# First attention: the keys' tiles of the score matmuls 128 columns wide as the stationary operand in place of 126

## The chip, the cores and the metric

The kernel is one program on one core of a Trainium2 chip. The metric is the time of one execution on the device in microseconds (us); lower is better. It was run three times before the change.

## What is computed

Two gated layers of a Flamingo-like block on 8 sequences of 256 tokens (T = 2,048 queries, 256 wide) that attend to 8 x 1,601 = 12,808 context tokens, with 16 heads of 16 dimensions:

```python
x = x + tanh(g_xattn[0]) * L0_xattn(layernorm(x), ctx)
x = x + tanh(g_ffn[0])   * L0_ffn(layernorm(x))      # experts, top 2
x = x + tanh(g_xattn[1]) * L1_xattn(layernorm(x), ctx)
x = x + tanh(g_ffn[1])   * L1_ffn(layernorm(x))
```

The change lies in `L0_xattn`, in which every query of all sequences sees all 12,808 keys:

```python
q, k, v = fq_sym(q * scale, -1), fq_sym(k, -1), fq_sym(v, 2)   # int8 steps
attn = einsum('bhqd,bhkd->bhqk', q, k)
attn = fq_unsigned(softmax(attn), -1)    # rounded to max/255
out  = einsum('bhqk,bhkd->bhqd', attn, v)
```

Rounding to the row's maximum/255 makes the exact maximum of each row of scores necessary before the exponentials: exp(score - maximum + ln 255) is then the unrounded step, and adding 1024 in a 16-bit float rounds it.

## The kernel before, in words

The program goes through its stages one after the other: projections and quantization of queries, keys and values, the first attention (`first_attention`, lines 792 to 1211), its output projection, the first feed-forward layer, the second attention and the second feed-forward layer. Only the first attention is touched.

It goes through 16 heads and, for each, two chunks of 1,024 queries: 32 bodies, written out four at a time (`IB` = 4), the first four flat and the others in a loop `Fori(1, LOOPS)` with `LOOPS` = 8, so seven turns. Within a body the keys are cut into `NE` = 102 tiles of `KT` = 126, the last of 82. The operands:

- `Kb` (`a_K`): keys in bf16, 112 rows (dimensions and their parts), two halves for two heads, 12,808 columns each. Rows 0 to 53 (`E_ROWS`) serve the scores for the exponentials, with six rows that subtract the row's maximum; rows 64 to 111 (`M_ROWS`) serve the scores for the maximum.
- `Qb` (`a_Q`): queries in the same rows, four chunks.
- `e` (`a_e`), `p` (`a_p`): exponentials in fp32 and rounded in fp16, rings of 8 tiles of 126 keys x 1,024 queries.

Work of one step s (one tile of keys), by engine:

- TensorE: two score matmuls (`e_half`, L1047): the tile of keys is stationary, 54 rows x 126 columns, and 512 queries move, one PSUM bank each. Between them one maximum piece each (`m_piece`, L1064): 128 queries stationary, 48 rows, and 512 keys move, for the maximum of the body after. Then the output matmuls of the tile four steps back (`av`): four with the values stationary (L1087, 32 columns, column tiles of the array) and four with `sel` (L1091), which sum the exponentials in fp32.
- VectorE: one reduction to the maximum of each piece (L1180), 200 whole ones and a short one (L1183) a body; then the maximum over them (L1191). The pieces have three PSUM banks.
- ScalarE: one exponential over 1,024 queries (L1151) for each tile.
- GpSimd: the rounding (L918) for each tile; once a body, at step `SPLIT` = 93, six small operations that split the maximum in bf16 parts (L900 to L910).

The order on TensorE is a list that is built once (lines 855 to 873) and issued for each body: for each half of a step the score matmul, then as many pieces as are due (201 over 204 slots, so three slots have none), and behind the second half the output matmuls that are owed. Steps 4 and 5 have no output matmuls, steps 6 and 7 have two tiles of them. After step `TURN` = 98 eight transposes (L1073) turn the next body's maxima, which ScalarE copies to `Qb` (L1136). Waits: a score half waits until the exponential two tiles back is done, since scores have two pairs of banks (L1046); a piece waits for the reduction three pieces back (L1062); output matmuls wait for the rounding (L1080); the first of a body waits for ScalarE's copy of the previous body's output (L1083, L1132).

Before the first piece TensorE waits for GpSimd's four memsets (L879 to L883, `init`).

Of the kernel before, what the change touches and what calls it, by code (L numbers as in the profile page):

```python
# [8 lines left out]
BF16 = mybir.dt.bfloat16  # L9
# [5 lines left out]
P = 128  # L15
BANK = 512
HEADS = 16
HD = 16
# [19 lines left out]
M_AT, IROWS = 2 * HD, 6  # L38
E_ROWS = 3 * HD + IROWS
M_ROWS = slice(64, 64 + 3 * HD)  # L40
# [45 lines left out]
class Kernel:  # L86
# [705 lines left out]
    def first_attention(self):  # L792


        nc, sh = self.nc, self.sh
        NE, NM, NC, KT, QC, QT, PIECES = sh.NE, sh.NM, sh.NC, sh.KT, sh.QC, sh.QT, sh.PIECES
# [10 lines left out]
        LN255 = math.log(255.0)  # L807
        K_DMAS, Q_DMAS, O_DMAS = 9, 6, 8
        with ExitStack() as ctx:
            Kb = self.sb(ctx, "a_K", [M_ROWS.stop, 2, sh.NK], BF16)  # L810
            Qb = self.sb(ctx, "a_Q", [M_ROWS.stop, 4, QC], BF16)
            Vb = self.sb(ctx, "a_V", [P, 2, sh.KTILES, 2 * HD], F16)
            skb = self.sb(ctx, "a_sk", [P, 2, sh.KTILES])
# [9 lines left out]
            init = self.sem(ctx, "a_init")  # L823

            ld_k = [self.sem(ctx, f"k_loaded{b}") for b in range(2)]
# [15 lines left out]
            def e_bank(i, s):  # L841

                return 2 * ((i + s + (s > TURN)) % 2)
# [6 lines left out]
            def key_rows(t):  # L850
                return sh.KLAST if t == sh.KTILES - 1 else KT
# [6 lines left out]
            for slot in range(2 * NE):  # L858
                s, y = divmod(slot, 2)
# [15 lines left out]
            @block.gpsimd  # L875
            def _(g):
                for s in self.early_sems:
                    g.sem_clear(s)
                g.memset(mparts[:, :, :], 0.0).then_inc(init, 1)  # L879
                g.memset(sel[:, 0:HD], 0.0).then_inc(init, 1)  # L880
                g.memset(sel[:, HD:2 * HD], 1.0).then_inc(init, 1)
                g.wait_ge(init, 3)
                g.memset(p[96:P, :, :], SHIFT).then_inc(init, 1)  # L883
                g.wait_ge(init, 4)

                def held(sem, value):
                    g.wait_ge(sem, value)
                    g.sem_inc(pool_held, 1)

                def split(it, ii, first=False):  # L890

                    n, hb, t0 = it * IB + ii, (ii // NC) % 2, (ii % NC) * QT
                    c = n * LINKS
                    cols = mparts[:, :, M_AT:M_AT + IROWS].rearrange("p t (a b) -> p t a b", b=2)
                    hi, mid, lo = cols[:, :, 0:3, 0], cols[:, :, 0:2, 1], cols[:, :, 2, 1]
                    held(ld_k[hb], 16 * K_DMAS * (it + ii // NC // 2 + 1))
                    held(m_ready, n + 1)
                    if not first:
                        held(m_turned, n)
                    g.tensor_tensor(ms[:, 1, :], ms[:, 0, :], sqb[:, hb, t0:t0 + QT], ALU.mult).then_inc(chain, 1)  # L900
                    held(chain, c + 1)
                    g.tensor_scalar(ms[:, 2, :], ms[:, 1, :], -1.0, LN255, ALU.mult, ALU.add).then_inc(chain, 1)
                    held(chain, c + 2)
                    g.tensor_copy(hi, along(ms[:, 2, :], 2, 3)).then_inc(chain, 1)
                    held(chain, c + 3)
                    g.tensor_tensor(ms[:, 3, :], ms[:, 2, :], hi[:, :, 0], ALU.subtract).then_inc(chain, 1)
                    held(chain, c + 4)
                    g.tensor_copy(mid, along(ms[:, 3, :], 2, 2)).then_inc(chain, 1)
                    held(chain, c + 5)
                    g.tensor_tensor(lo, ms[:, 3, :], mid[:, :, 0], ALU.subtract).then_inc(m_split, 1)  # L910
                    held(m_split, n + 1)

                def body(it, i):
                    for s in range(NE):
                        kk = i * NE + s
                        rows = key_rows(s)
                        held(exp_done, it * (IB * NE) + kk + 1)
                        g.tensor_scalar(p[0:rows, kk % RE, :], e[0:rows, kk % RE, :], 1.0, SHIFT,  # L918
                                        ALU.mult, ALU.add).then_inc(rounded, 1)
                        if s == SPLIT:  # L920
                            held(rounded, it * (IB * NE) + kk + 1)
                            split(it, i + 1)
                split(0, 0, True)
                for i in range(IB):
                    body(0, i)
                with g.Fori(1, LOOPS) as it:
                    for i in range(IB):
                        body(it, i)
# [4 lines left out]

            def load_k(sp, h, b, at):
                row, part = (M_KEYS + E_KEYS)[at]
                sp.dma_start(Kb[row:row + HD, b, :], self.d_k0[part, h]).then_inc(ld_k[b], 16)

            def load_inv(sp, h, b):
                sp.dma_start(Kb[M_AT:M_AT + IROWS, b, :], self.d_inv[h]).then_inc(ld_k[b], 16)

            def load_v(sp, h, b, at):
                r = slice(at * P // V_DMAS, (at + 1) * P // V_DMAS)
# [94 lines left out]
            def _(pe):  # L1037
                def e_half(g, i, s, y, first_body):
                    n, kk = g * IB + i, i * NE + s
                    if y == 0:  # L1040
                        if s == 0:
                            pe.wait_ge(m_rows, n + 1)
                        if s == TURN + 2:
                            pe.wait_ge(m_rows, n + 2)
                        elif not (first_body and kk < 2):
                            pe.wait_ge(exp_done, g * (IB * NE) + kk - (s != TURN + 1))  # L1046
                    last = pe.matmul(self.PS[0:key_rows(s), e_bank(i, s) + y, :], Kb[0:E_ROWS, (i // NC) % 2, s * KT:s * KT + key_rows(s)],  # L1047
                                     Qb[0:E_ROWS, i % 4, y * BANK:(y + 1) * BANK], start=True, stop=True)
                    if y == 1:
                        last.then_inc(scores_e, 1)  # L1050
# [57 lines left out]
                        elif not first_body:  # L1108
                            av(g - 1, IB - 1, op[2], False)

                pe.wait_ge(init, 4)
                for j in range(NM):
                    m_piece(0, 0, 0, j, True)
                m_turn(0, -1, 2)
# [10 lines left out]
            @block.scalar  # L1125
            def _(a):
                def gather(n, b, o_used):

                    a.wait_ge(av_done, (n + 1) * NE)
                    if o_used is not None:  # L1130
                        a.wait_ge(o_stored[b], o_used)
                    a.activation(og[:, b, :], self.PS[:, O_BANK, 0:QW], ACT.Copy).then_inc(gathered, 1)  # L1132

                def rows(n, b, bank):
                    a.wait_ge(m_turned, n + 1)
                    a.activation(Qb[M_AT:M_AT + IROWS, b, :], self.PS[M_AT:M_AT + IROWS, bank, :].bitcast(BF16),  # L1136
                                 ACT.Copy).then_inc(m_rows, 1)

                def body(g, i, first_body):
                    n = g * IB + i  # L1140
                    hb = i // NC
                    for s in range(NE):
                        kk = i * NE + s
                        if s == 0 and i % NC == 0:
                            a.wait_ge(ld_k[hb], 16 * K_DMAS * (g + 1))
                        a.wait_ge(scores_e, g * (IB * NE) + kk + 1)
                        if s % 2 == 0 and not (first_body and kk < RE):

                            a.wait_ge(av_done, g * (IB * NE) + kk - RE + 2)
                        r = key_rows(s)  # L1150
                        a.activation(e[0:r, kk % RE, :], self.PS[0:r, e_bank(i, s):e_bank(i, s) + 2, :], ACT.Exp,  # L1151
                                     scale=skb[0:r, hb, s:s + 1]).then_inc(exp_done, 1)

                        if s == LAG + 1 and not (first_body and i == 0):
                            if first_body and i <= 2:
                                gather(n - 1, (i - 1) % 2, None)
                            elif i > 0:
                                gather(n - 1, (i - 1) % 2, 8 * O_DMAS * (g * IB + i - 1 - (i - 1) % 2))
                            else:
                                gather(n - 1, (IB - 1) % 2, 8 * O_DMAS * (g * IB - 1 - (IB - 1) % 2))  # L1160
                        if s == TURN:
                            rows(n + 1, (i + 1) % 4, t_bank(i))

                a.wait_ge(init, 4)
                rows(0, 0, 2)
                for i in range(IB):
                    body(0, i, True)
                with a.Fori(1, LOOPS) as g:
                    for i in range(IB):
                        body(g, i, False)  # L1170
                gather(LOOPS * IB - 1, (IB - 1) % 2, 8 * O_DMAS * (LOOPS * IB - 1 - (IB - 1) % 2))
# [1291 lines left out]
```

## Time and profile before

| what | value |
|---|---|
| median of 3 runs | 6643.13 us (6642.96 to 6648.73) |
| profiled execution, own time | 6652.62 us |
| its span | 6650.8 us |
| mean granted TensorE clock | 0.921 |
| TensorE matmul / weight load busy | 5788.3 / 2456.0 us (87% / 37%) |
| VectorE busy | 5609.7 us (84%) |
| ScalarE busy | 4504.5 us (68%) |
| GpSimd busy | 3781.9 us (57%) |

The profile is of one execution. PE is TensorE's matmuls, PEld its weight loads, which can run beside matmuls; DVE is VectorE, ACT ScalarE, POOL GpSimd, SP the engine that issues the DMAs. Busy shares are averages over stages with different limits; matmuls are pipelined and their ends are modelled, so their starts tell more than their durations. Idle time of an engine that is not waited for costs nothing. A granted clock of 1.00 is 2.4 GHz, 0.50 is 1.2 GHz.

### The profile page before, as it was taken

The page shows a single profiled execution, that of the slowest core. Times are in us where ns is not written, and L with a number is a line of the kernel's source. Part 1 is how long each engine was busy: PE and PEld are TensorE (multiplying, and loading weights), DVE is VectorE, ACT ScalarE, POOL GpSimd, SP SyncE. Part 2 cuts the span into 40 slices and gives each one's busy share as a digit, 9 for nine tenths or more (in the row PEclk, how much of TensorE's full clock was granted, in tenths as well). Part 3 has the DMA queues.
Part 4 walks back from the last instruction along what each step waited for, and adds up shares of the span by engine and source line. Part 5 has one row for each costly group of instructions (what it writes and reads, how often), then busy time and mean ns, then how long its engine had stood idle before and what let it go on. Part 6 is the DMA issues. An engine that isn't in the chain of part 4 may idle for free. (4 is left out here: it accounts for less than half of the span.)

```text
span 6650.8 us, 180101 instructions
## 1 busy us (share of the span) xinstructions
PE 5788.3 (87%) x64160; PEld 2456.0 (37%) x64160; DVE 5609.7 (84%) x8987; ACT 4504.5 (68%) x4373; POOL 3781.9 (57%) x4001
## 2 busy tenths in 40 slices
PE   2865999999999999999999999999978577999824
PEld 2651233333333333333333333333344353544412
DVE  4877999999999899899989999989963646777786
ACT  0650598898898889888989988988842012666512
POOL 2330488888788788788878878878840001000021
PEclk7995799999999999999999999999989787999966
DMA  1544101101101001011011010010110068777700
GB/s 58 131 115 126 18 9 23 21 8 27 18 11 25 15 16 25 7 24 21 8 27 18 11 25 15 16 23 9 22 37 0 10 267 222 114 110 111 112 28 11
DMA packets 176565, 315.50 MB, mean 47 GB/s; under 512 B 91731, under 2 KB 137812, under 8 KB 171042
## 3 DMA queue, kind: packets, MB, share of 16 engines
q1 hardware_dynamic: 175656, 303.45, 21.3%
q8 instruction: 561, 9.19, 0.6%
q14 instruction: 348, 2.85, 0.2%
HBM read 192.39 MB, written 113.07 MB: 46 GB/s over the span
## 5 line engine op out<-in xcount | busy, mean ns | idle before, releaser
L1180 DVE TENSOR_REDUCE a_mx<-PS 128x1 f32<-128x512 f32 x6620 | 4073.1, 686 | 240.3 <-PE PS L1064 236.7
L1151 ACT ACTIVATE a_e<-PS,a_sk 126x1024 f32<-126x1024 f32 x3264 | 3634.0, 1114 | 494.5 <-PE PS L1047 146.0
L918 POOL TENSOR_SCALAR a_p<-a_e 126x1024 f16<-126x1024 f32 x3264 | 3413.4, 1046 | 681.7 <-ACT a_e L1151 628.6
L1047 PE MATMUL PS<-a_Q,a_K 54*126 54x512 bf16 x6528 | 2112.3, 404 | 31.9 <-issue 22.7
L1064 PE MATMUL PS<-a_K,a_Q 48*128 48x512 bf16 (+1 forms) x6884 | 2108.7, 383 | 31.1 <-POOL a_p L883 30.8
L1091 PE MATMUL PS<-a_e,a_sel 126*32 126x256 f32 x26112 | 1996.2, 382 | 28.1 <-issue 28.1
L1047 PEld LDWEIGHTS PS<-a_Q,a_K 54*126 54x126 bf16 x6528 | 615.3, 131 | 1383.8 <-issue 1325.1
L1087 PE MATMUL PS<-a_p,a_V 128*32 128x256 f16 x13056 | 960.4, 284 | 14.3 <-ACT a_og L1132 10.3
L1087 PEld LDWEIGHTS PS<-a_p,a_V 128*32 128x32 f16 x13056 | 336.8, 93 | 1251.5 <-POOL a_p L918 1053.5
L1091 PEld LDWEIGHTS PS<-a_e,a_sel 126*32 126x32 f32 x26112 | 756.4, 110 | 38.3 <-issue 32.0
L2137 DVE TENSOR_REDUCE b_mx<-PS 128x1 f32<-128x512 f32 x803 | 504.6, 685 | 188.1 <-PE PS L2021 188.0
L2111 ACT ACTIVATE b_e<-PS 128x1024 f32<-128x1024 f32 (+1 forms) x416 | 415.7, 1024 | 223.6 <-PE PS L2041 220.9
L1064 PEld LDWEIGHTS PS<-a_K,a_Q 48*128 48x128 bf16 x6884 | 404.3, 94 | 167.0 <-DVE a_mx L1180 129.4
L2187 POOL TENSOR_SCALAR b_ms<-b_ms 128x8 f32<-128x8 f32 x33 | 7.7, 233 | 631.0 <-DVE b_ms L2148 631.0
L2021 PE MATMUL PS<-b_K,b_Q 96*128 96x512 bf16 (+1 forms) x1070 | 279.8, 346 | 50.1 <-POOL b_K L2172 41.1
L2041 PE MATMUL PS<-b_Q,b_K 99*128 99x256 bf16 (+1 forms) x1664 | 256.0, 277 | 15.4 <-ACT b_e L2111 9.5
L486 PE MATMUL PS<-wkv,cT 128*126 128x256 f32 (+1 forms) x816 | 207.5, 386 | 47.7 <-DVEq L551 47.7
L2056 PE MATMUL PS<-b_e,b_V 128*32 128x256 f32 (+1 forms) x3328 | 229.1, 388 | 9.0 <-ACT b_og L2096 6.6
L1807 POOL MEMSET v1v<- 128x6656 f32 x2 | 11.2, 5646 | 378.8 <-POOLq L1734 378.8
L1846 ACT ACTIVATE k1f<-PS,bk 128x512 f32<-128x512 f32 x64 | 36.3, 593 | 269.5 <-PE PS L1821 269.5
L2041 PEld LDWEIGHTS PS<-b_Q,b_K 99*128 99x128 bf16 (+1 forms) x1664 | 142.2, 99 | 162.2 <-ACT b_e L2111 79.1
L1136 ACT ACTIVATE a_Q<-PS 6x1024 bf16<-6x1024 bf16 x33 | 33.5, 1016 | 242.0 <-PE PS L1073 241.2
(321 smaller groups left out, 3522.1 us busy)
## 6 DMA issues: line engine op xcount, KB each, us to landing
b_K<-d_k SPq DMA_DIRECT2D x210, 200.1 KB, 6.3
a_K<-d_k SPq DMA_DIRECT2D x99, 400.2 KB
d_v<-v1v SPq DMA_DIRECT2D x9, 3328.0 KB, 10.3
b_V<-d_v SPq DMA_DIRECT2D x36, 832.0 KB, 12.4
d_k<-k_T SPq DMA_DIRECT2D x100, 252.0 KB, 4.0
d_k<-k1p SPq DMA_DIRECT2D x54, 400.2 KB, 6.9
a_V<-d_v SPq DMA_DIRECT2D x68, 204.0 KB, 2.8
d_v<-vq SPq DMA_DIRECT2D x17, 803.2 KB
```

Source lines behind the costliest of these rows:

```text
L918: g.tensor_scalar(p[0:rows, kk % RE, :], e[0:rows, kk % RE, :], 1.0, SHIFT, ALU.mult, ALU.add).then_inc(rounded, 1)
L1047: last = pe.matmul(self.PS[0:key_rows(s), e_bank(i, s) + y, :], Kb[0:E_ROWS, (i // NC) % 2, s * KT:s * KT + key_rows(s)], Qb[0:E_ROWS, i % ...
L1064: last = pe.matmul(self.PS[:, M_BANK + j % sh.SLOTS, c0:c0 + wd], Qb[M_ROWS, ii % 4, t * P:(t + 1) * P], Kb[M_ROWS, (ii // NC) % 2, k0:k0 ...
L1087: pe.matmul(self.PS[32 * j:32 * j + 32, O_BANK, 0:QW], Vb[:, i // NC, t, :], p[:, kk % RE, j * QW:(j + 1) * QW], start=(t == 0), stop=Fals ...
L1091: last = pe.matmul(self.PS[32 * j:32 * j + 32, O_BANK, 0:QW], sel[0:key_rows(t), :], e[0:key_rows(t), kk % RE, j * QW:(j + 1) * QW], start ...
L1151: a.activation(e[0:r, kk % RE, :], self.PS[0:r, e_bank(i, s):e_bank(i, s) + 2, :], ACT.Exp, scale=skb[0:r, hb, s:s + 1]).then_inc(exp_done, 1)
L1180: v.tensor_reduce(mx[:, col:col + 1], bank, AX.X, ALU.max).then_inc(max_done, 1)
L2021: last = pe.matmul(self.PS[:, M_BANK + j % SLOTS, c0:c0 + wd], Qb[0:ROWS, ii % SETS, tq * P:(tq + 1) * P], Kb[0:ROWS, ii % SETS, hh, k0:k0 ...
L2041: last = pe.matmul(self.PS[0:rows, e_bank(s) + j // 2, (j % 2) * LQ:(j % 2 + 1) * LQ], Kb[0:ROWS + MROWS, i % SETS, j, s * P:s * P + rows] ...
L2056: last = pe.matmul(self.PS[32 * j:32 * j + 32, O_BANK, 0:LQ], Vb[0:rows, i // 4, s, i % 4 * QH + j, :], e[0:rows, k % RE, j * LQ:(j + 1) * ...
L2111: a.activation(e[0:r, kk % RE, :], self.PS[0:r, e_bank(s):e_bank(s) + 2, :].rearrange("p b n -> p (b n)"), ACT.Exp).then_inc(exp_done, 1)
L2137: v.tensor_reduce(mx[:, col:col + 1], bank, AX.X, ALU.max).then_inc(max_done, 1)
```

## The change

`Kb` becomes 46 columns longer in each half (`PAD` = 102 x 126 + 128 - 126 - 12,808), GpSimd clears these columns in rows 0 to 53 at the start, and each score matmul takes 128 columns from the tile's first key on, so two more than the tile has, and writes all 128 rows of its PSUM bank. The two further columns are the first two keys of the tile behind, or cleared ones; for the last tile there are 46 further columns. ScalarE, GpSimd and the sum over the exponentials go on with 126 rows (82 for the last tile) and do not read the further rows. The tiles still start 126 keys apart. The loads of keys fill the first 12,808 columns of a half, as before.

```diff
@@ -807,7 +807,8 @@
-            Kb = self.sb(ctx, "a_K", [M_ROWS.stop, 2, sh.NK], BF16)
+            PAD = sh.KTILES * KT + P - KT - sh.NK
+            Kb = self.sb(ctx, "a_K", [M_ROWS.stop, 2, sh.NK + PAD], BF16)
...
@@ -881,7 +882,8 @@
                 g.memset(p[96:P, :, :], SHIFT).then_inc(init, 1)
-                g.wait_ge(init, 4)
+                g.memset(Kb[0:E_ROWS, :, sh.NK:sh.NK + PAD], 0.0).then_inc(init, 1)
+                g.wait_ge(init, 5)
...
@@ -933,10 +935,10 @@
-                sp.dma_start(Kb[row:row + HD, b, :], self.d_k0[part, h]).then_inc(ld_k[b], 16)
+                sp.dma_start(Kb[row:row + HD, b, 0:sh.NK], self.d_k0[part, h]).then_inc(ld_k[b], 16)
...
-                sp.dma_start(Kb[M_AT:M_AT + IROWS, b, :], self.d_inv[h]).then_inc(ld_k[b], 16)
+                sp.dma_start(Kb[M_AT:M_AT + IROWS, b, 0:sh.NK], self.d_inv[h]).then_inc(ld_k[b], 16)
...
@@ -1044,7 +1046,7 @@
-                    last = pe.matmul(self.PS[0:key_rows(s), e_bank(i, s) + y, :], Kb[0:E_ROWS, (i // NC) % 2, s * KT:s * KT + key_rows(s)],
+                    last = pe.matmul(self.PS[:, e_bank(i, s) + y, :], Kb[0:E_ROWS, (i // NC) % 2, s * KT:s * KT + P],
                                      Qb[0:E_ROWS, i % 4, y * BANK:(y + 1) * BANK], start=True, stop=True)
...
-                pe.wait_ge(init, 4)
+                pe.wait_ge(init, 5)
...
-                a.wait_ge(init, 4)
+                a.wait_ge(init, 5)
```

No instruction changes its place. On TensorE, one regular step in the first flat body, before the change:

```order
L1047 MATMUL PS<-a_Q,a_K 126x512
L1064 MATMUL PS<-a_K,a_Q 128x512
L1047 MATMUL PS<-a_Q,a_K 126x512
L1064 MATMUL PS<-a_K,a_Q 128x512
L1087 MATMUL PS<-a_p,a_V 32x256 x4
L1091 MATMUL PS<-a_e,a_sel 32x256 x4
```

and with it (the lines lie two further down):

```order
L1049 MATMUL PS<-a_Q,a_K 128x512
L1066 MATMUL PS<-a_K,a_Q 128x512
L1049 MATMUL PS<-a_Q,a_K 128x512
L1066 MATMUL PS<-a_K,a_Q 128x512
L1089 MATMUL PS<-a_p,a_V 32x256 x4
L1093 MATMUL PS<-a_e,a_sel 32x256 x4
```

Only the width of the score matmuls' output differs. On GpSimd one memset is new, at the start of the stage, with the change:

```order
L880 MEMSET a_mparts 128x1024
L881 MEMSET a_sel 128x16
L882 MEMSET a_sel 128x16
L884 MEMSET a_p 32x8192
L885 MEMSET a_K 54x2x46
```

It comes last of the five, ahead of the wait that TensorE shares.

## Rows read from the trace of the kernel before

**Rows 1.** The page, busy time of each engine.
```profile
PE 5788.3 (87%) x64160; PEld 2456.0 (37%) x64160; DVE 5609.7 (84%) x8987; ACT 4504.5 (68%) x4373; POOL 3781.9 (57%) x4001
```
**Rows 2.** The page, costliest groups: line engine op count | busy us, mean ns | idle.
```profile
L1180 DVE TENSOR_REDUCE a_mx<-PS 128x1 f32<-128x512 f32 x6620 | 4073.1, 686 | 240.3 <-PE PS L1064 236.7
L1151 ACT ACTIVATE a_e<-PS,a_sk 126x1024 f32<-126x1024 f32 x3264 | 3634.0, 1114 | 494.5 <-PE PS L1047 146.0
L918 POOL TENSOR_SCALAR a_p<-a_e 126x1024 f16<-126x1024 f32 x3264 | 3413.4, 1046 | 681.7 <-ACT a_e L1151 628.6
```
**Rows 3.** Timeline (start us, us, what), weight loads of first halves nine steps apart.
```profile
3000.51 0.13 PEld L1047 LDWEIGHTS PS<-a_Q,a_K 54*126 54x126 bf16 x1 [0.41 <-issue]
...
3011.56 0.13 PEld L1047 LDWEIGHTS PS<-a_Q,a_K 54*126 54x126 bf16 x1 [0.41 <-issue]
```
**Rows 4.** Timeline of POOL, roundings with a backlog behind the split.
```profile
1889.61 4.42 POOL L918 TENSOR_SCALAR a_p<-a_e 126x1024 f16<-126x1024 f32 x4 [0.35 <-POOL a_mparts L910]
```
**Rows 5.** Timeline of DVE at the stage's start and over one body.
```profile
689.61 26.39 DVE L1180 TENSOR_REDUCE a_mx<-PS 128x1 f32<-128x512 f32 x44
...
1614.59 0.37 DVE L1191 TENSOR_REDUCE a_ms<-a_mx 128x8 f32<-128x208 f32 x1
...
1639.79 31.40 DVE L1180 TENSOR_REDUCE a_mx<-PS 128x1 f32<-128x512 f32 x51 [0.48 <-PE PS L1064]
...
1742.06 0.37 DVE L1191 TENSOR_REDUCE a_ms<-a_mx 128x8 f32<-128x208 f32 x1
```
**Rows 6.** Waits, 1600 to 4700 us: total us, times, longest.
```profile
DVE a_mx L1180 <- PE PS L1064: 169.3, 187, 6.3
...
PEld PS L1064 <- DVE a_mx L1180: 16.5, 46, 0.4
```
**Rows 7.** Timeline of PE, maximum pieces: a step with one, the next.
```profile
1937.14 0.39 PE L1064 MATMUL PS<-a_K,a_Q 48*128 48x512 bf16 x1
...
1938.37 0.60 PE L1064 MATMUL PS<-a_K,a_Q 48*128 48x512 bf16 x2
```
**Rows 8.** Timeline of PE: the 82-key step of a body, then the next step.
```profile
1894.11 0.41 PE L1047 MATMUL PS<-a_Q,a_K 54*82 54x512 bf16 x1
...
1894.66 0.29 PE L1087 MATMUL PS<-a_p,a_V 128*32 128x256 f16 x4
...
1895.32 0.43 PE L1047 MATMUL PS<-a_Q,a_K 54*126 54x512 bf16 x1
1895.32 0.60 PE L1064 MATMUL PS<-a_K,a_Q 48*128 48x512 bf16 x2
1895.58 0.38 PE L1047 MATMUL PS<-a_Q,a_K 54*126 54x512 bf16 x1
1895.89 0.29 PE L1087 MATMUL PS<-a_p,a_V 128*32 128x256 f16 x4
```
**Rows 9.** Groups by shape, 1600 to 5000 us: weight loads, busy us, mean ns.
```profile
L1047 PEld LDWEIGHTS PS<-a_Q,a_K 54*126 54x126 bf16 x5092 | 481.1, 131 | 1085.5 <-issue 1042.0 <-ACT a_e L1151 43.5
L1064 PEld LDWEIGHTS PS<-a_K,a_Q 48*128 48x128 bf16 x5250 | 301.8, 94 | 20.2 <-DVE a_mx L1180 17.2
...
L1047 PEld LDWEIGHTS PS<-a_Q,a_K 54*82 54x82 bf16 x52 | 3.9, 112 | 10.7 <-issue 10.7
```
**Rows 10.** Timeline of PE: steps 4 and 5, and the second half of step 8.
```profile
1900.50 0.78 PE L1047 MATMUL PS<-a_Q,a_K 54*126 54x512 bf16 x2
...
1906.69 0.38 PE L1047 MATMUL PS<-a_Q,a_K 54*126 54x512 bf16 x1
```
**Rows 11.** Timeline of POOL at the stage's start, a small memset.
```profile
588.54 0.11 POOL L881 MEMSET a_sel<- 128x16 f32 x1
```
**Rows 12.** Busy us (count) of PE, PEld, DVE, ACT, POOL in ten us; granted clock.
```profile
2028.00:2038.00 10.00, 9.39 (x98) 3.50 (x96) 7.29 (x13) 6.62 (x8) 7.01 (x8) 0.83 0.31 50
```

## The prediction, made before the changed kernel was run

> **What bounds the kernel now.** I read the page first: the tensor engine is busy 87% of the span, VectorE 84%, ScalarE 68% and GpSimd 57% [rows 1]. Averages do not say who waits for whom, so I went on to the groups of instructions, then the waits, then the timeline of one step. The changed matmul has its whole life in the first attention, from about 720 to 4,900 us. There are 32 bodies there (16 heads, two chunks of queries each) with 102 steps each, 3,264 in all, the count of the exponentials [rows 2].
>
> In a regular step the first halves start at 3000.51 and, nine steps on, at 3011.56: 11.05/9 = 1.228 us per step [rows 3]. What sets 1.228?
> - Not ScalarE: its exponential takes 1.114 us [rows 2], so 0.11 us of each step is left.
> - Not GpSimd: its rounding takes 1.046 us [rows 2]. Where it has a backlog, four of them take 4.42 us, which is (4.42 - 1.05)/3 = 1.12 us from start to start [rows 4].
> - Hardly VectorE, but it is close. At the start, where only it and the pieces run, 44 reductions take 26.39 us, its own pace: less the last one's 0.69 that is 25.70/43 = 0.598 each [rows 5]. Two per step are 1.196. In the regular stretch 51 take 31.40, so (31.40 - 0.69)/50 = 0.614, two of them 1.228: the step, not its own pace. In 3,100 us the maximum pieces' weight loads wait for VectorE for 16.5 us in total, while VectorE waits 169.3 us for their matmuls [rows 6].
> - So it is the tensor engine. A step with one maximum piece less is no shorter: from 1937.14 to 1938.37 it is 1.23 us [rows 7]. The maximum pieces are therefore not in the chain; the score matmuls and the eight output matmuls behind them are.
>
> **Where in the step the stationary operand counts.** One step in order of time [rows 8]: the first score half of step s starts at 1895.32 and lasts 0.43, the second half starts at 1895.58 and lasts 0.38, the output matmuls come at 1895.89. The second half is 0.05 shorter than the first because its weights come in behind the first half; the first half shows its own load, since nothing was loaded ahead of it. The last tile of a body has 82 keys and is a natural experiment: from its first half to the output matmuls it takes 1894.66 - 1894.11 = 0.55 us, against 0.57 with 126 keys [rows 8]. The load itself takes 112 ns with 82 columns and 131 with 126 [rows 9]: 19 ns, 0.43 ns a column, and the step follows by 0.02, as far as the rows resolve it. The exposed load moves the step one for one.
>
> **What the change does to it.** The maximum pieces load 128 columns of the same type in 94 ns [rows 9]. They have more columns and take 37 ns less than 126: a full 128 is loaded in another, faster way. I take it that the score loads, 54 rows high and now 128 wide, take about 94 ns too. The Trainium skill has this as Fast Weight Load ("TensorE: Matmul & The Clock Gate", section Weight-path perf modes): on for exactly 128 columns that aren't fp32; by that rule the two rows agree. The same page's section on LDWEIGHTS gives the columns divided by 1.2 GHz, 105 ns for 126; with its factor of about two for the fast way an estimate of 52 ns saved a step and 160 us in all. The rows show 37 ns, and the rows decide.
>
> Three ceilings on what a step can give back:
> 1. the load: 131 - 94 = 0.037 us;
> 2. the maximum pieces run beside the scores on other rows of the array. Their pair starts at 1895.32 and ends 0.60 later, at 1895.92, the scores' second half at 1895.58 + 0.38 = 1895.96 [rows 8]: the output matmuls, which need the whole array, can come 0.04 earlier before the pieces hold them up;
> 3. VectorE at two reductions: 1.228 - 1.196 = 0.032 us.
>
> The third is the lowest; VectorE has spare time at three slots a body without a piece, so it does not bind hard. I take 0.032 a step, a step of 1.196.
>
> The number of steps. From one body's maximum to the next it is 1742.06 - 1614.59 = 127.47 us [rows 5]. Steps 5 to 8 (no output work, then twice two tiles of it) go from 1900.50 (a row of two second halves, the first of which is step 4's) to 1906.69, 6.19 us for 4 steps [rows 10]; they wait for ScalarE. The other 98 take 121.28, 0.92 more than 98 x 1.228; that is the step that waits for the exponential and the turn of the maxima. So 97 regular steps a body, 3,104 in all, less an allowance of five behind each of the loop's seven jumps back, where the engine starts anew and whose saving I put at nothing: 3,070. **Sum:** 3,070 x 0.032 = 98 us. In steps 7 and 8 and behind the turn the load stands behind a wait and shows too: 3 x 32 x 0.035 = 3 us. Off go the last tiles, which have 0.019 already: 32 x 0.019 = 0.6 us. GpSimd's new memset (54 rows x 92 elements) stands ahead of the first piece; the small memset before it takes 0.11 us [rows 11], so +0.1. Together -101 us.
>
> At nothing I put: the two more rows of scores (nobody reads them; ScalarE and GpSimd keep 126 rows), the loads of keys (same bytes, another length of row), the shift of what lies behind the keys in memory. The cover of ScalarE shrinks from 0.11 to 0.08 us a step, GpSimd's from 0.11 to 0.07: both still stand. With the tensor engine faster, VectorE is next, at once.
>
> The profiled execution took 6652.6 us, 9.5 over the median of 6643.1. It would be 6551.6; the median becomes 6643.1 - 101 = **6542**.
>
> **Rivals.**
> - *The load stays slow.* Tiles of keys start every 252 bytes, and the second head's half now starts 92 bytes later; the fast loads in the trace start at whole multiples of 256 bytes. If the fast way needs that, 128 columns cost 2 x 0.43 ns more: 3,070 x 0.0009 = +3 us, 6646. The 128-column rows [rows 9] speak against it, but nothing in the trace shows a fast load at such a start. The Trainium skill ("TensorE: Matmul & The Clock Gate", section LDWEIGHTS) has the load grow with the columns, which gives this case too, a hair slower. Chance 0.09.
> - *Half the gain.* Two fast loads, of scores and of pieces, meet at the start of a step and one waits for the other, or VectorE falls behind more often than three empty slots make good. Then 0.02 of 0.037 remains: 3,070 x 0.02 + 4 = 65 us, 6578. Against it: today the slow load and the fast one start together and the fast one still takes 94. Chance 0.10.
> - *Slower.* Today the second half's load lies behind the first half. If a fast load of the scores cannot run while the other rows' matmul streams, it shows with its 0.094 us and the step is 1.228 - 0.037 + 0.094 = 1.285: +0.057 x 3,070 = +175 us, 6818. It decides as soon as more than 0.037 a step shows. Against it: the pieces' second load is fast and lies behind a matmul today, and their pair takes only 0.60 [rows 8]. Chance 0.04.
>
> The tensor clock: from 2028 to 2038 us, around steps 5 to 8 of a body, where the engine idles, the granted clock was 0.83 on average [rows 12], so 3.4 us of 10 at the lower level, 1.2 GHz, which cost at most 1.7 us of work. Five such dips more or fewer in 32 bodies would be 8 us either way; that goes into the range.
>
> **How the numbers follow.** Forecast 0.77, half 0.10, slow load 0.09, slower 0.04. The forecast's own range is 6524 (the whole 0.037 and two or three clock dips fewer: 3,070 x 0.037 + 5) to 6556 (0.027 a step); with the half-gain case and some clock it reaches 6585; the slow-load and slower cases, 0.13, are left out. Within 0.2% (13 us, about what a measurement of this kernel can tell from no change) is the slow load's case: 0.09. Faster is 0.87, slower 0.04.
>
> **What would show it.** Right: the score loads at about 94 ns; the first half of a step at 0.39 in place of 0.43; nine steps in 10.8 us; a body of about 124.3 us; VectorE's waits for pieces fewer, the pieces' loads waiting for VectorE more. Wrong: loads at 131 (slow load), loads at 94 with steps at 1.228 (the load was not in the chain), output matmuls later behind the second half (slower).

## The result, and the profile after

| what | before | after |
|---|---|---|
| median of 4 runs, same chip | 6645.93 us (6642.96 to 6651.25) | 6531.79 us (6530.62 to 6536.08) |
| ratio, 95% interval | | 0.9829 [0.9812, 0.9846] |
| profiled execution, own time | 6652.62 us | 6530.62 us |
| its span | 6650.8 us | 6528.6 us |
| mean granted TensorE clock | 0.921 | 0.923 |

Faster by 114 us, with the interval by 102 to 125. The forecast was 101 and 6542, the range 6524 to 6585. The page after, busy time of each engine and its costliest groups:

```profile
PE 5668.4 (87%) x64160; PEld 2228.2 (34%) x64160; DVE 5520.5 (85%) x8987; ACT 4504.5 (69%) x4373; POOL 3787.3 (58%) x4002
...
L1182 DVE TENSOR_REDUCE a_mx<-PS 128x1 f32<-128x512 f32 x6620 | 3985.0, 682 | 212.4 <-PE PS L1066 208.8
L1153 ACT ACTIVATE a_e<-PS,a_sk 126x1024 f32<-126x1024 f32 x3264 | 3633.9, 1114 | 377.9 <-PE PS L1049 128.5
L920 POOL TENSOR_SCALAR a_p<-a_e 126x1024 f16<-126x1024 f32 x3264 | 3418.4, 1047 | 560.0 <-ACT a_e L1153 180.7
```

The work of ScalarE and GpSimd is the same to 0.2% [rows 2]; the idle time ahead of it fell by 116.6 and 121.7 us. That is the same time seen twice: both engines follow TensorE and wait less often. Now the loads that were to become fast, grouped by shape over 1600 to 4600 us of the kernel after:

```profile
L1066 PEld LDWEIGHTS PS<-a_K,a_Q 48*128 48x128 bf16 x4898 | 283.6, 94 | 31.4 <-DVE a_mx L1182 18.1
L1049 PEld LDWEIGHTS PS<-a_Q,a_K 54*128 54x128 bf16 x4808 | 272.4, 94 | 1025.8 <-issue 980.8 <-ACT a_e L1153 45.0
```

94 ns for the scores' load, as for the pieces', against 131 before [rows 9]. Nine steps, by the loads of first halves (timeline of PEld, after):

```profile
2948.76 0.09 PEld L1049 LDWEIGHTS PS<-a_Q,a_K 54*128 54x128 bf16 x1 [0.41 <-issue]
...
2959.53 0.09 PEld L1049 LDWEIGHTS PS<-a_Q,a_K 54*128 54x128 bf16 x1 [0.41 <-issue]
```

10.77/9 = 1.197 us a step against 1.228 [rows 3]. Inside a step (timeline of PE, after):

```profile
2951.16 0.39 PE L1049 MATMUL PS<-a_Q,a_K 54*128 54x512 bf16 x1
2951.16 0.39 PE L1066 MATMUL PS<-a_K,a_Q 48*128 48x512 bf16 x1
2951.38 0.38 PE L1049 MATMUL PS<-a_Q,a_K 54*128 54x512 bf16 x1
2951.39 0.38 PE L1066 MATMUL PS<-a_K,a_Q 48*128 48x512 bf16 x1
2951.70 0.29 PE L1089 MATMUL PS<-a_p,a_V 128*32 128x256 f16 x4
```

The first half is 0.39 where it was 0.43 [rows 8]. The second now starts 0.22 behind it, where it was 0.26, and the output matmuls come 0.54 behind it, where they came 0.57. One body by the maxima over it (timeline of DVE, after):

```profile
1852.33 0.37 DVE L1193 TENSOR_REDUCE a_ms<-a_mx 128x8 f32<-128x208 f32 x1
...
1976.65 0.37 DVE L1193 TENSOR_REDUCE a_ms<-a_mx 128x8 f32<-128x208 f32 x1
```

124.32 us against 127.47 [rows 5], 3.15 a body.

**Where the 122 us between the two profiled executions lie.** Read by the first and the last score matmul of the stage: the program up to the first score is 1.5 us shorter, what follows the stage 3.9, the stage itself 116.8. Of these, 32 bodies by 3.15 are 101. The other 16 are in less regular places. The stretches at the half level of the granted clock (1.2 GHz) that begin between 740 and 4,700 us add up to 112.6 us before, in 12 stretches, and to 71.7 us after, in 8: before, five bodies away from the loop's jumps have one of 3.4 us, after it two. Such a stretch makes its body about 1.5 us longer (129.0 against 127.47 before). Whether the change does that, or the execution, is taken up below.

### The profile page after: what moved, and what is told of

Its sections match the earlier page's. It is cut to its first block and busy times, and to the rows that moved or that the text cites. A ratio compares the mean times of both kernels' runs of the same rounds, so it can differ in the third digit from the quotient of the medians.

```text
span 6528.6 us, 180102 instructions
## 1 busy us (share of the span) xinstructions
PE 5668.4 (87%) x64160; PEld 2228.2 (34%) x64160; DVE 5520.5 (85%) x8987; ACT 4504.5 (69%) x4373; POOL 3787.3 (58%) x4002
## 5 line engine op out<-in xcount | busy, mean ns | idle before, releaser
L1182 DVE TENSOR_REDUCE a_mx<-PS 128x1 f32<-128x512 f32 x6620 | 3985.0, 682 | 212.4 <-PE PS L1066 208.8
L1093 PE MATMUL PS<-a_e,a_sel 126*32 126x256 f32 x26112 | 1988.8, 381 | 29.2 <-issue 29.2
L1049 PE MATMUL PS<-a_Q,a_K 54*128 54x512 bf16 x6528 | 1976.7, 383 | 32.9 <-issue 23.6
L1049 PEld LDWEIGHTS PS<-a_Q,a_K 54*128 54x128 bf16 x6528 | 369.3, 94 | 1383.3 <-issue 1320.7
L1093 PEld LDWEIGHTS PS<-a_e,a_sel 126*32 126x32 f32 x26112 | 754.7, 110 | 38.0 <-issue 31.2
```

The lines of the kernel that those rows point to most:

```text
L1049: last = pe.matmul(self.PS[:, e_bank(i, s) + y, :], Kb[0:E_ROWS, (i // NC) % 2, s * KT:s * KT + P], Qb[0:E_ROWS, i % 4, y * BANK:(y + 1) * ...
L1093: last = pe.matmul(self.PS[32 * j:32 * j + 32, O_BANK, 0:QW], sel[0:key_rows(t), :], e[0:key_rows(t), kk % RE, j * QW:(j + 1) * QW], start ...
L1182: v.tensor_reduce(mx[:, col:col + 1], bank, AX.X, ALU.max).then_inc(max_done, 1)
```

## The experiments

Unless an edit says otherwise, an experiment starts from the kernel after. Lines are those of its own kernel. "Step" is the median over nine steps in a row from 1,500 to 4,600 us, divided by nine, "body" the median of the bodies away from the jumps; before they are 1.228 and 127.47, after 1.196 and 124.32. "Half clock" is the sum of the stretches at 1.2 GHz that begin between 740 and 4,700 us.

### The layout alone, and 127 columns

`w126_layout` has the longer `Kb` and the new memset, and scores over the tile's own columns:

```diff
-                    last = pe.matmul(self.PS[:, e_bank(i, s) + y, :], Kb[0:E_ROWS, (i // NC) % 2, s * KT:s * KT + P],
+                    last = pe.matmul(self.PS[0:key_rows(s), e_bank(i, s) + y, :], Kb[0:E_ROWS, (i // NC) % 2, s * KT:s * KT + key_rows(s)],
```

> The keys' tile in its new, longer layout and the new memset, but score matmuls of 126 columns (82 in the last tile) as before. Theory (the gain is the weight load of 128 columns alone): load 131 ns, step 1.228 us, the time of the kernel before, 6643 to 6646 us. Rival (the other start addresses of the keys, or what lies behind them, give the gain): step at or near 1.196, about 6532 us; a part of both would lie between.

Measured: 6643.82 us against 6644.39, ratio 0.9999 [0.9989, 1.0009], step 1.228.

`w127` takes one of the two columns only, `self.PS[0:127, …]` and `s * KT:s * KT + 127`.

> Changed kernel with 127 columns in place of 128. Theory (a full 128 is loaded in another way, and 127 is not): load about 131.5 ns, step 1.228 to 1.229 us, 6643 to 6648 us. Rival (the gain comes from writing nearly all rows, or from the width being near 128): load near 94 ns, step 1.196, about 6532 us.

Measured: 6653.39 us, ratio 1.0013 [1.0004, 1.0023], step 1.230, body 127.65, so 0.18 more and 6 us over 32 bodies. The time is 5 us above the theory's range. Their loads, grouped by shape over 1600 to 4600 us; the layout's alone:

```profile
L1049 PEld LDWEIGHTS PS<-a_Q,a_K 54*126 54x126 bf16 x4636 | 437.0, 131 | 988.3 <-issue 947.9 <-ACT a_e L1153 40.4
```

and with 127:

```profile
L1049 PEld LDWEIGHTS PS<-a_Q,a_K 54*127 54x127 bf16 x4680 | 447.0, 132 | 998.3 <-issue 956.7 <-ACT a_e L1153 41.6
```

What follows: nothing of the gain comes from the layout, and one column more than 126 makes the load 1 ns and the step 2 ns longer. Of the widths tried, only the full 128 is fast. The Trainium skill ("TensorE: Matmul & The Clock Gate", section Weight-path perf modes) asks for exactly 128 weights that aren't fp32; by that rule, the two loads agree.

### Which of the two loads counts

`first128` widens only the first half's operand, `second128` only the second's (`y == 1`):

```diff
-                    last = pe.matmul(self.PS[:, e_bank(i, s) + y, :], Kb[0:E_ROWS, (i // NC) % 2, s * KT:s * KT + P],
+                    w = P if y == 0 else key_rows(s)
+                    last = pe.matmul(self.PS[0:w, e_bank(i, s) + y, :], Kb[0:E_ROWS, (i // NC) % 2, s * KT:s * KT + w],
```

> Only the first score half of each step loads 128 columns; the second half keeps 126 (82 in the last tile). Theory (only the first half's load shows, the second's lies behind the first half's matmul): the step is that of the changed kernel, 1.195 to 1.197 us, about 6532 us. Rival (both loads count, or the gain needs both to be fast): the step lies between, about 1.212, about 6580 us, or stays at 1.228.

Measured: 6535.3 us against 6644.32, ratio 0.9836 [0.9821, 0.9851], step 1.196, body 124.32. Its loads:

```profile
L1050 PEld LDWEIGHTS PS<-a_Q,a_K 54*126 54x126 bf16 x2381 | 339.0, 142 | 0.0
L1050 PEld LDWEIGHTS PS<-a_Q,a_K 54*128 54x128 bf16 x2405 | 222.9, 93 | 1024.6 <-issue 980.4 <-ACT a_e L1154 44.2
```

> Only the second score half loads 128 columns; the first keeps 126 (82 in the last tile). Theory (the first half's load is the one that shows): load of the second half 95 ns, step still 1.228 us, about 6644 us. Rival (both count): step about 1.212 us, about 6590 us.

Measured: 6646.42 us, ratio 1.0001 [0.9992, 1.0011], step 1.228, body 127.5. Its loads:

```profile
L1050 PEld LDWEIGHTS PS<-a_Q,a_K 54*128 54x128 bf16 x2341 | 327.4, 140 | 0.0
L1050 PEld LDWEIGHTS PS<-a_Q,a_K 54*126 54x126 bf16 x2318 | 298.1, 129 | 990.3 <-issue 949.1 <-ACT a_e L1154 41.3
```

The idle column tells it in each: the second half's load has no idle time ahead of it, it follows the first's and lies beside the first half's matmul. Fast or slow, it leaves the step where it was. The gain is the first half's load, the first behind the output matmuls: 0.41 us after the load ahead of it, with its matmul right behind. One row I had not expected: the second half's 128 columns show 140 ns, not 95, where the first half's load is a slow one.

### Fewer columns

If the step follows the first load, narrower tiles must shorten it by the slow way's slope too. `w72`, `w96` and `w112` take 72, 96 and 112 columns; the rows of scores beyond them are not computed, so these kernels leave out part of the sum of exponentials and of the output (`w72` also fills `p` from row 64). The edit, for 112:

```diff
-                return sh.KLAST if t == sh.KTILES - 1 else KT
+                return min(112, sh.KLAST) if t == sh.KTILES - 1 else 112
...
-                    last = pe.matmul(self.PS[:, e_bank(i, s) + y, :], Kb[0:E_ROWS, (i // NC) % 2, s * KT:s * KT + P],
+                    last = pe.matmul(self.PS[0:112, e_bank(i, s) + y, :], Kb[0:E_ROWS, (i // NC) % 2, s * KT:s * KT + 112],
```

> Score tiles of 72 columns, slow load: scores, exponentials, rounding and sums of rows 72 and up of each tile are left out, the count of instructions and their lengths along the queries stay. Theory (the exposed load moves the step one for one, 0.43 ns a column): load 131 - 54 x 0.43 = 108 ns, step 1.228 - 0.023 = 1.205 us, 3,100 x 0.023 = 71 us less than before, about 6574 us. Rival (only the fast way frees something else, such as the path on which the pieces' weights come in; the load's length doesn't matter): step 1.228, 6643 us.

Measured: 9699.15 us, ratio 1.4597 [1.4573, 1.4622]. Neither theory had this. The granted clock over the span in 40 slices, after and then `w72`:

```profile
PEclk7995799999999999999999999999979797999956
```

```profile
PEclk8955555555555555555555555555555559789976
```

and two first halves one step apart in `w72` (timeline of PE):

```profile
3000.57 0.64 PE L1049 MATMUL PS<-a_Q,a_K 54*72 54x512 bf16 x1
...
3002.76 0.64 PE L1049 MATMUL PS<-a_Q,a_K 54*72 54x512 bf16 x1
```

The step is 2.19 us, and the clock stays at the lower level for the whole stage. The run says nothing of the slope; it says that the same number of instructions over narrower tiles did not get the full clock back. The columns of the score matmuls are not all that is narrower: the four matmuls with `sel` behind them have 72 rows in place of 126 (L1093), as they have 112 and 96 in the two runs below. No run separates columns from rows.

> Score tiles of 112 columns by the slow way; rows 112 and up of each tile are left out of scores, exponentials, rounding and sums. Theory (the exposed load moves the step one for one, 0.43 ns a column): load 131 - 14 x 0.43 = 125 ns, step 1.228 - 0.006 = 1.222 us, 3,100 x 0.006 = 19 us less, about 6627 us. Rival (a slow load's length doesn't move the step): 1.228, 6645. The run with 72 columns stood at the half clock throughout; if the narrower tiles do that here too, the step will be near 2.2 us, and the clock, not the load, decides the time.

Measured: 6638.55 us against 6644.32, ratio 0.9991 [0.9982, 1.0000]. Its loads:

```profile
L1049 PEld LDWEIGHTS PS<-a_Q,a_K 54*112 54x112 bf16 x4682 | 415.2, 125 | 1003.7 <-issue 963.8 <-ACT a_e L1153 40.0
```

Load 6 ns shorter, step 1.2225, so 5.8 ns shorter, body 126.9: the slope as foretold, about 0.41 ns a column. But the time fell by 6 us, not by 19. The half clock shows where it went: 129.7 us of it, against 112.6 before and 85.3 in the layout's kernel, and 23.9 us at a stretch behind three of the jumps, where the kernel before had at most 20.5. It is not one execution alone: the mean granted clock is 0.919 to 0.921 in all ten runs, and 0.921 to 0.924 in the 21 of the kernel before beside them.

> Between the runs with 112 and 72 columns, with the same kind of omission (rows 96 and up of each tile). Theory (the load's length moves the step, and a narrower tile makes the granted clock give way more easily): load 131 - 30 x 0.43 = 118 ns and a step of 1.215 us where the clock is full, so 3,100 x 0.013 = 40 us less than 6645; but stretches at the half clock behind the jumps and in the bodies' starts grow further than with 112, and take back some or all of it: 6610 to 6700 us. If the clock stays at half for good, as with 72, the step is about 2.2 and the time about 9,700. Rival (the clock with 72 fell for another cause than the width): no more half clock than with 112, 6615 us.

Measured: 7086.77 us (7039.73 and 7133.8, two runs), ratio 1.0667 [1.0500, 1.0835], above what either theory had. Its profiled run, loads of first halves nine steps apart in a stretch at full clock:

```profile
3300.97 0.12 PEld L1049 LDWEIGHTS PS<-a_Q,a_K 54*96 54x96 bf16 x1 [0.41 <-issue]
...
3311.91 0.12 PEld L1049 LDWEIGHTS PS<-a_Q,a_K 54*96 54x96 bf16 x1 [0.41 <-issue]
```

10.94/9 = 1.216: at full clock the step is 0.012 shorter than with 126 columns, 0.41 ns a column again. And two windows of the same run (us, busy us and counts of PE, PEld, DVE, ACT, POOL, granted clock, DMA share, GB/s):

```profile
1758.00:2007.00 249.00, 247.87 (x1868) 69.30 (x1868) 146.61 (x230) 129.53 (x119) 121.24 (x122) 0.52 0.08 16
3300.00:3400.00 100.00, 100.00 (x1322) 33.38 (x1314) 98.48 (x163) 90.85 (x82) 85.28 (x82) 1.00 0.02 5
```

The engine is all but never idle in either, and one has half the clock in nearly all of it: the stretch at the lower level begins at 1,747 us, behind a jump, and ends at 1,996. Its 249 us are longer than a body even at that pace (the last two bodies take 226.6 us each, by the maxima). Over the stage the mean clock is 0.86 (731 to 5,380 us). So the theory of the slope holds at full clock for 126, 112 and 96 columns, and what the narrow tiles cost is time at the lower clock.

### What holds the step at 1.196

The text called VectorE the lowest ceiling. `red448` takes 64 columns off each reduction, so the maxima are over part of the keys, and 8 off the exponent so that nothing overflows:

```diff
-                    g.tensor_scalar(ms[:, 2, :], ms[:, 1, :], -1.0, LN255, ALU.mult, ALU.add).then_inc(chain, 1)
+                    g.tensor_scalar(ms[:, 2, :], ms[:, 1, :], -1.0, LN255 - 8.0, ALU.mult, ALU.add).then_inc(chain, 1)
...
-                        v.tensor_reduce(mx[:, col:col + 1], bank, AX.X, ALU.max).then_inc(max_done, 1)
+                        v.tensor_reduce(mx[:, col:col + 1], bank[:, 0:448], AX.X, ALU.max).then_inc(max_done, 1)
```

> Changed kernel with reductions over 448 of each piece's 512 scores (64 of 512 keys are left out of the maximum, and 8 is taken off the exponent so that it stays finite). VectorE's own pace falls from 0.598 to about 0.598 - 64/960 MHz = 0.53 us, two are 1.06. Theory A (the step of 1.196 is set by VectorE's two reductions): the step falls to what TensorE's chain allows. Theory B (TensorE's chain gives 1.196 by itself, since the pieces' second matmul now ends last ahead of the output matmuls): the step stays at 1.195 to 1.197, the time falls only by what the places behind the turn and the empty slots give, under 15 us, so 6517 to 6532 us. If A, a step of 1.19 or less and below 6515.

Measured: 6519.9 us against 6646.39, ratio 0.9811 [0.9794, 0.9827]. One body of it (timeline of DVE):

```profile
1839.60 0.37 DVE L1193 TENSOR_REDUCE a_ms<-a_mx 128x8 f32<-128x208 f32 x1
...
1963.92 0.37 DVE L1193 TENSOR_REDUCE a_ms<-a_mx 128x8 f32<-128x208 f32 x1
```

124.32 again, to the hundredth, with the step at 1.196. VectorE does not hold it. The 12 us come from the stage's start, where only the pieces run and VectorE is the bound: the first score stands at 717.4 us in place of 729.4. `red448_126`, the same two edits in the kernel before, splits this off:

> Kernel before (126 columns) with reductions over 448 of 512, same omission. Theory (the kernel before is set by TensorE's chain with the exposed load): step 1.228 still, 6630 to 6646 us. Rival (VectorE's reductions set a part of it): step below 1.225 and a time below 6630.

Measured: 6634.44 us, ratio 0.9983 [0.9973, 0.9992], step 1.228; first score at 715.5 us in place of 731.0. The gain is 12 us by the medians in both pairs; the first score moved by 12.1 us in one and 15.5 in the other, single executions each. It is the start's, with either operand.

`piece448` adds to `red448` pieces that are 448 wide on TensorE too:

```diff
+                        wd = min(wd, 448)
```

> As the run with reductions over 448, and the pieces' matmuls are 448 wide too (64/2.4 GHz = 27 ns shorter each); the scores stay 512 wide. Theory (the pieces' second matmul is the last ahead of the output matmuls, 5 ns behind the scores' second half): the step falls by about 5 ns to 1.191, since the scores' pair takes over; 3,100 x 0.005 = 15 us below the run with 448 reductions alone. Rival (the scores' pair is the last in any case): no difference between the two.

Measured: 6524.54 us, ratio 0.9817 [0.9801, 0.9833]. Three steps of it (timeline of PE):

```profile
1880.42 0.39 PE L1049 MATMUL PS<-a_Q,a_K 54*128 54x512 bf16 x1
1880.42 0.55 PE L1067 MATMUL PS<-a_K,a_Q 48*128 48x448 bf16 x2
...
1883.99 0.39 PE L1049 MATMUL PS<-a_Q,a_K 54*128 54x512 bf16 x1
```

3.57/3 = 1.190; the step is 1.1917, 4.6 ns less than with whole pieces. The starts of the traces, read in whole ns (medians from 1,500 to 4,600 us), say what the output matmuls follow. The second column is the start of the piece's second matmul behind that of the second score half; the others are by how much the first output matmul starts ahead of the modelled end of each:

| kernel | second piece behind second half | ahead of the piece's end | ahead of the half's end |
|---|---|---|---|
| before | -34 | 36 | 70 |
| after, `first128`, `red448` | 3 | 70 | 66 |
| `piece448` | -23 | 20 | 70 |

The output matmuls stand 70 ns ahead of whichever of the two ends last. Before the change that was the score half, with the piece 34 ns earlier; after it, it is the piece, by 4 ns; with narrower pieces it is the score half again. So at 1.196 the second ceiling holds the step. Over the stage 4.6 ns a step should have given 14 us, and the time is 4.6 us above that of `red448`. The granted clock takes it back: half clock is 109.2 us against 68.3, in 16 stretches against 8, with some bodies of 125.4 between those of 123.8, and the mean granted clock is 0.919 to 0.920 in all four runs, 0.923 to 0.925 in those of `red448`.

### Output matmuls of two tiles together

If each turn between the score matmuls and the output matmuls costs the tensor engine a load with nothing beside it, half as many turns should cost less. `pairs128` holds back the output matmuls of every other step:

```diff
+                    if s % 2 or s == LAG + 2:
+                        order += owed
+                        owed = []
```

> Changed kernel, order only: the output matmuls of two tiles are issued together behind every odd step in place of one tile behind each step. Before and behind the output matmuls the timeline shows about 0.09 us in which nothing streams; pairs save one such change over in each two steps. Theory (TensorE's chain is the bound and VectorE right behind it): TensorE would need about 1.10 a step, VectorE keeps it at 1.196, the empty slots and the places behind the turn are caught up: 1 to 2 us a body, 6470 to 6500 us. Rival (bursts: the two pairs of score banks and three banks of pieces are too few, ScalarE and VectorE run dry while two tiles of output matmuls run, 1.0 us): step above 1.196, slower than 6532.

Measured: 6966.54 us, ratio 1.0482 [1.0465, 1.0500]. The rival's case: two steps take 2.70 us. First halves and the output matmuls (timeline of PE):

```profile
2999.96 0.39 PE L1050 MATMUL PS<-a_Q,a_K 54*128 54x512 bf16 x1
...
3001.46 0.29 PE L1090 MATMUL PS<-a_p,a_V 128*32 128x256 f16 x4
...
3002.66 0.39 PE L1050 MATMUL PS<-a_Q,a_K 54*128 54x512 bf16 x1
```

and the load of the fourth piece (PEld):

```profile
3001.14 0.09 PEld L1067 LDWEIGHTS PS<-a_K,a_Q 48*128 48x128 bf16 x1 [0.64 <-DVE a_mx L1183]
```

Four pieces in a row need four banks, and there are three. The fourth waits 0.64 us for VectorE, and the output matmuls stand behind it on TensorE, in order. Without that wait the pair would have taken 2.70 - 0.64 = 2.06 us by these rows; a fourth bank was not tried, and VectorE's own 2 x 1.196 a pair would hold it above that.

### The idle place of each body

Steps 5 to 8 are 6.12 us in the kernel after, 1.3 more than four regular steps: no output matmuls in steps 4 and 5, two tiles of them in 6 and 7. `early128` moves ScalarE's copy of the previous body's output ahead of the exponential of step 4 (it was behind that of step 5), so that its banks come free, and starts the output matmuls one step earlier:

```diff
-                    owed += [("av", 0, t) for t in range(NE) if max(t + LAG, LAG + 2 + t // 2) == s]
+                    owed += [("av", 0, t) for t in range(NE) if max(t + LAG, LAG + 1 + (t + 1) // 2) == s]
...
+                        if s == LAG and not (first_body and i == 0):
...
-                        if s == LAG + 1 and not (first_body and i == 0):
```

> Changed kernel, with the copy of the previous body's output (ScalarE) ahead of the exponential of step 4 in place of behind that of step 5, and the first output matmuls one step earlier (tile 0 behind step 5, tiles 1 and 2 behind 6, tile 3 behind 7). Theory (from step 4's to step 8's second half the changed kernel takes 6.12 us where four steps of 1.196 are 4.78, since TensorE waits for that copy): the stretch shortens by about 1 us a body to 5.2, and the granted clock dips there less; 32 us and some 5 us of clock, about 6495 us, a body of 123.3 us. Rival (ScalarE becomes the bound behind step 4, or VectorE with its pieces): less than 10 us of gain, above 6522.

Measured: 6503.03 us (6497.9 to 6508.3, five runs) against 6644.32, ratio 0.9790 [0.9777, 0.9804]. The first halves of steps 4 to 8 (timeline of PE), `early128`:

```profile
1860.18 0.39 PE L1049 MATMUL PS<-a_Q,a_K 54*128 54x512 bf16 x1
...
1860.80 0.39 PE L1049 MATMUL PS<-a_Q,a_K 54*128 54x512 bf16 x1
...
1862.34 0.39 PE L1049 MATMUL PS<-a_Q,a_K 54*128 54x512 bf16 x1
...
1864.08 0.39 PE L1049 MATMUL PS<-a_Q,a_K 54*128 54x512 bf16 x1
...
1865.28 0.39 PE L1049 MATMUL PS<-a_Q,a_K 54*128 54x512 bf16 x1
```

and the kernel after:

```profile
1870.46 0.39 PE L1049 MATMUL PS<-a_Q,a_K 54*128 54x512 bf16 x1
...
1871.07 0.39 PE L1049 MATMUL PS<-a_Q,a_K 54*128 54x512 bf16 x1
...
1872.27 0.39 PE L1049 MATMUL PS<-a_Q,a_K 54*128 54x512 bf16 x1 [0.24 <-ACT a_e L1153]
...
1874.84 0.39 PE L1049 MATMUL PS<-a_Q,a_K 54*128 54x512 bf16 x1
...
1876.58 0.39 PE L1049 MATMUL PS<-a_Q,a_K 54*128 54x512 bf16 x1
```

5.10 us against 6.12, the body 123.28 against 124.32: 32 x 1.04 = 33 us by the traces, about 29 by the medians. The two kernels were timed against the same kernel before in different comparisons, not against each other; their intervals [0.9777, 0.9804] and [0.9812, 0.9846] do not meet. (`first128`, timed beside it, took 6535.3.) This is the fastest version here.

## Why the prediction was right, point by point

- **The load becomes fast: right.** 131 to 94 ns. Starts every 252 bytes do not hinder it, so the first rival falls. `w127` shows that a width of nearly 128 does not do.
- **The load of the first half alone moves the step, one for one: right.** `first128` has all of it and `second128` none; at full clock 126, 112 and 96 columns give 1.228, 1.2225 and 1.216, 0.41 ns a column, where the text had 0.43, the slope read from the one tile of 82 keys [rows 9].
- **A step of 1.196: the number right, its cause wrong.** The text said "The third is the lowest" and "With the tensor engine faster, VectorE is next, at once". Of the load's 37 ns a step gave back 32 (1.2283 to 1.1963); the second ceiling, the pieces' pair, stops it there, as `red448` and `piece448` show between them (in `piece448` it gave back 36.6). The text read that ceiling from rows with two digits as 0.04, so above VectorE's 0.032; in whole ns the piece was only 34 ns ahead. That VectorE's 1.228 - 1.196 gave the same 0.032 is luck. VectorE's share, 2 x 0.598, was a duration per piece read at the stage's start, and in `red448` a body is the same without that load. Of the signs that the text named, VectorE's waits for pieces did become fewer, but the pieces' loads wait for VectorE hardly more; waits from 1600 to 4600 us, after:

```profile
DVE a_mx L1182 <- PE PS L1066: 145.7, 185, 6.3
...
PEld PS L1066 <- DVE a_mx L1182: 18.1, 48, 0.4
```

  The loads' 18.1 us fall in 3000/124.32 = 24.1 bodies, against 16.5 in 3100/127.47 = 24.3 [rows 6]: 0.75 us a body against 0.68. VectorE's are 6.0 us a body against 7.0.
- **The body: right.** 124.32 against "about 124.3", the first half 0.39, nine steps 10.77 against 10.8.
- **Half the gain, and slower: neither came.** The fast loads of scores and pieces start together and both take 94 ns; the second half's load stays behind the first half's matmul.
- **The memset: 0.17 us, not 0.1.** GpSimd, after:

```profile
593.92 0.17 POOL L885 MEMSET a_K<- 54x92 bf16 x1
```

- **The sum: 101 forecast, 114 measured, 102 to 125 with the interval.** The step's term is what it said, 3.15 a body. What the sum lacks is 13 us, and the clock, which it had in the range only, is where the traces show a part of them. Beside the profiled layout's kernel, whose own time of 6640.28 us lies below its median of 6643.82 where that of the profiled kernel before lies 7 us above its own, the stage after is 106.3 us shorter: 101, and 5.5 more with 13.6 us less half clock. How much of the clock is the change's doing stays open. Half clock in the kernels with a fast first load is 71.7 us (after), 64.9 (`first128`), 68.3 (`red448`), 71.7 (`early128`), 85.3 (`pairs128`) and 109.2 (`piece448`); in those with 126 columns there, 112.6 (before), 85.3 (layout), 88.7 (`second128`) and 85.3 (`red448_126`). That looks like the load, but `w127`, with a slow load and no gain, has 71.7 too. No run separates the two.
- **Two slips without weight.** 121.28 is 0.94 more than 98 x 1.228, not 0.92; and seven turns have six jumps back, which the bodies of 138 us and more show, so the allowance for steps behind them was five too large, 0.2 us.

## What to carry to other kernels

Look for weight loads with a gap ahead of them and their matmul right behind, here at the first matmul behind a burst of another tiling: in this kernel only that one was in the chain. Padding its operand to the full 128 columns, with whatever lies next to it, was worth more than having two columns fewer. When two engines come within a percent of each other after a change, name the ceilings one by one and take each away before saying which one holds; sums that agree don't tell. And read the granted clock beside the step: with narrower pieces and with 112 columns the step became shorter and more time at half clock took most or all of it back.

## What the runs showed of the hardware that was not expected

- The granted clock fell, and stayed low, while TensorE was busy. With score tiles of 72 keys it stayed at 1.2 GHz for the whole stage, 9699 us; with 96 it came and went, 7087 us; with 112 some stretches were longer; the numbers of instructions are the same in all. In the window of `w96` at half clock PE is busy 247.87 of 249 us. The Trainium skill ("TensorE: Matmul & The Clock Gate", section What's actually happening) has the clock follow how busy the engine is; by that rule this window would be at full clock, and the measurement decides against it here.
- A slow load took 112, 125, 131 and 132 ns with 82, 112, 126 and 127 columns (means of 1600 to 4600 us and more, nearly all at full clock); one of 128 took 94.
- Where a load of 126 and one of 128 columns follow each other in a step, the second shows 140 to 142 ns, whichever of the two it is; between equal ones it is within 4 ns of the first (128 and 132 before, 93 and 96 after, medians). Its cause was not tried.
